# Nine of 49 destination blocks gathered, row turns in a layer's first steps, row stores on ScalarE's queue

## The chip, the cores and the metric

The kernel runs on one core of a Trainium2 chip. The metric is device time in microseconds, from the first to the last instruction of the program and what lies around them.

## What is computed

Four graph networks in a row over one graph of 6250 nodes (128 features) and 100000 edges, each behind a layer norm with relu and added to its input. The parts that matter here are the sums over edges:

```python
# L0: 2 layers, batch norm:   pooled = segment_sum(h[src'], dst', 6250) * inv_deg
# L1 ("sage"), 4 layers:
agg = jax.ops.segment_sum(h[src], dst, num_segments=N_NODES)
agg = agg / jnp.maximum(deg, 1.0)[:, None]
h = h @ Ws + agg @ Wn + b            # relu but in the last layer
# L2 ("plain" sum), 1 layer: messages = concat(nodes[senders], edge_attr) @ W_message.T
aggregated = jax.ops.segment_sum(messages, receivers, num_segments=n_nodes)
# L3 ("conv"), 2 layers, with self loops:
agg = jax.ops.segment_sum(ew[:, None] * (h @ W)[s], d, num_segments=n); h = elu(agg + b)
```

## The kernel before

The nodes are 49 blocks of 128 (NS), 6272 columns. `build_tables` writes a table of edge counts (8-bit, source block by source lane by destination) to memory. A sum over edges is then a dense product: the rows of the source nodes, split in two 16-bit parts (`rows`, kept on the chip), times the table's columns. L1, L2 and L3 do this in `layer_chain` (L2019), called three times: kind "sage" with L = 4 layers, "plain" with 1 and "conv" with 2. L0 runs outside it.

*Dense part.* Destinations are cut into strips of US = 7 blocks, 896 columns, done as two halves of 448 in banks 0 and 1 (`acc`). DENSE = 6 strips take the dense path. A strip goes through the 49 source blocks in 14 pieces (`PIECES`, 4 and 3 blocks in turn). `dense_piece` waits for the piece's DMA and does, for both halves, for each block, for both parts one product at L2139: 14 pieces are 196 products. SP loads pieces into a ring of five buffers (`load_piece`), each as its buffer comes free.

*Gathered part.* The last US = 7 blocks (from GB0 = 42) don't use the table. For each block there is a list of its edges' sources (`glist`), and a unit is a third of a block's list: GpSimd issues GH = 6 indirect DMAs (L2116), each fetching 128 rows of 512 bytes from `hrows`, a copy of the rows in memory, into one of two buffers (`grow`). VectorE writes a hot matrix for the unit (`hots`, L2278) that says to which of the 128 destinations each row belongs, also in two buffers. TensorE does 12 products of 128 columns (`gathered`, L2163) into banks 6 and 7. So there are 21 units (NGH) in a layer. `GATHER_AT` gives the strip and piece behind which a unit is done: pieces 1, 4, 7 and 10 of strips 1 to 5, and piece 13, the last, of strip 4. GpSimd waits for the unit two before to be used (`g_used`), and at a layer's start for all row stores (`hr_out`).

*What follows a strip.* VectorE takes a bank out (`leave_bank`, L2311, L2313), sage adds the own term that TensorE made in `own_term` (L2175, L2318), ScalarE writes the new features (`replace`, L2247). The gathered blocks are taken out in two portions of 4 and 3 blocks (`HALVES`, `LAST_S`), at strip 3 and at strip 5. Then the new rows for the next layer are made: `turn` (L2195) multiplies each block by the next weight, ScalarE writes the high part (`high`, L2238), VectorE the low part (`turned_in`, L2290). A strip is turned behind piece TURN_AT = 2 of the next strip (the last one: of the next layer's first strip), the gathered blocks behind piece 12 of strip 5. SP stores each strip's rows to `hrows` (`store_rows`, L1204) from its own queue, R + 2 = 7 pieces later than the turn.

All engines work through their own queues in order; the order is written out by hand, engine by engine. VectorE's order in a strip is: the previous strip's `turned_in`, then the hot matrices `units(s)[2:] + units(s + 1)[:2]`, then the portions, then `leave_bank` of the strip.

*Before a chain.* `split_rows` (L1208) makes the first rows. For sage and plain its SP queue loads the first five pieces and then stores the rows in four DMAs (`ROW_STORES`, 576 to 1024 KB). It is a block of its own: the next block, the chain, starts when all engines' queues are through. In sage, ScalarE loads a broadcast factor row of 3136 KB (`C<-factors`) once five pieces are used. For conv, `update_nodes` makes and stores the first rows, and the change leaves it alone.

Of the kernel before, what the change touches and what calls it, by code (L numbers as in the profile page):

```python
# [65 lines left out]
GB0 = (NU - 1) * US  # L66
# [4 lines left out]
NGH = GU * US  # L71
# [517 lines left out]
def build_tables(k):  # L589

    nc = k.nc
    with ExitStack() as own:
# [15 lines left out]
        excess = sb("excess_g", [P, US], F32)  # L608
# [12 lines left out]
        with nc.Block() as block:  # L621
# [29 lines left out]
            def _(dve):  # L651
# [36 lines left out]
                mine, after = (blocks[:, GB0 % 4 + i:GB0 % 4 + i + US] for i in range(2))  # L688
# [362 lines left out]
def product(k, terms, dst, func, bias, stats=False, tbuf=None, lists=False):  # L1051
# [3 lines left out]
    with nc.Block() as block:  # L1055
# [6 lines left out]
        if lists:  # L1062
            @block.gpsimd
            def _(pool):
# [3 lines left out]
                for n in range(US):  # L1068
# [85 lines left out]
def load_piece(k, sp, tbuf, s, i, slot=None):  # L1154
# [4 lines left out]
    sp.dma_start(tbuf[:, at:at + (hi - lo) * SU].rearrange("p (b u) -> p b u", u=SU),  # L1159
                 k.table[t * US + lo:t * US + hi, :, bass.ds(s * SU, SU)].rearrange("b l u -> l b u")  # L1160
# [47 lines left out]
def split_rows(k, v, over_src, at, weight, own, tbuf, keep, store=False):  # L1208
# [17 lines left out]
    with nc.Block() as block:  # L1226
        @block.sync
        def _(sp):
# [691 lines left out]
def elu_stage(k, sums, bias, dst, out=None):  # L1920
# [19 lines left out]
    with nc.Block() as block:  # L1940
# [26 lines left out]
        if out is not None:  # L1967
# [24 lines left out]
HALVES = [(0, 4), (4, US)]  # L1992
DENSE = NU - 1
LAST_S = NU - 1
CHUNKS = [(0, 0), (0, 1), (1, 0), (1, 1), (2, 0), (2, 1), (LAST_S, 0), (3, 0), (3, 1), (4, 0), (4, 1), (LAST_S, 1),
          (5, 0), (5, 1)]
TURNS = [0, 1, 2, 3, 4, LAST_S, 5]
TURN_AT, TURN_LAST_AT, OWN_AT = 2, 12, 12
GATHER_AT = {at: n for n, at in enumerate(sorted([(s, i) for s in range(1, DENSE) for i in (1, 4, 7, 10)] + [(4, 13)]))}


def chunk_of(s, q):

    if s < DENSE:
        return slice(s * STRIP + q * HALF, s * STRIP + (q + 1) * HALF)
    return slice((s * US + HALVES[q][0]) * P, (s * US + HALVES[q][1]) * P)


def chunk_width(s, q):

    return HALF if s < DENSE else (HALVES[q][1] - HALVES[q][0]) * P


def blocks_of(s, q):

    return [s * US + i for i in range(*HALVES[q])]


def layer_chain(k, kind, v, dst, layers, at_scale, tbuf, factor=None, out=None):  # L2019
# [5 lines left out]
    total, turns = L * DENSE * NH, (L - 1) * NU  # L2025
# [9 lines left out]
    turned = {(l, s): l * NU + j for l in range(L) for j, s in enumerate(TURNS)}  # L2035

    def count(l, s, q):

        return l * len(CHUNKS) + CHUNKS.index((s, q)) + 1

    def before(l, s, q):

        same = [(m, c[0]) for m in range(L) for c in CHUNKS if c[1] == q]
# [3 lines left out]
    def acc(s, q):  # L2047

        return k.bank[q if s < DENSE else 6 + q][:, 0:chunk_width(s, q)]

# [8 lines left out]
    def events(l, s):  # L2059

        first = (l, s - 1) if s else (l - 1, DENSE - 1)
        return ([first] if first[0] >= 0 else []) + ([(l, LAST_S)] if s == DENSE - 1 else [])

    with ExitStack() as own_space:
# [10 lines left out]
        with nc.Block() as block:  # L2075
            @block.sync
            def _(sp):
                stores = {}
                for l in range(L - 1):
                    for j, s in enumerate(TURNS):  # L2080
                        piece = (l * DENSE + DENSE - 1) * NH + TURN_LAST_AT if s == LAST_S else (
                            l * DENSE + s + 1) * NH + TURN_AT
                        stores[piece + R + 2] = (l, s)
                for n in range(R, total):
                    sp.wait_ge(used.h, used.at(n - R + 1))
                    load_piece(k, sp, tbuf, n // NH % DENSE, n % NH, n % R)
# [4 lines left out]
                for j, s in enumerate(TURNS if conv else ()):  # L2091
                    sp.wait_ge(o_copied.h, o_copied.at(2 * j + 2))
                    b1 = min((s + 1) * US, full)
                    sp.dma_start(out[s * STRIP:b1 * P, :].rearrange("(b p) f -> p b f", p=P),
                                 out_rows[:, s * US:b1, :]).then_inc(o_out.h, 16)
                    if s == LAST_S:
                        sp.dma_start(out[full * P:N, :], out_rows[0:N - full * P, full, :]).then_inc(o_out.h, 16)
                if conv:
                    sp.wait_ge(o_out.h, o_out.at(16 * (NU + 1)))

            @block.gpsimd
            def _(pool):
# [5 lines left out]
                for l in range(L):  # L2108
                    pool.wait_ge(hr_out.h, hr_out.at(16 * (len(ROW_STORES) + l * NU)))
# [11 lines left out]
            def _(pe):  # L2121
                T = nc.tensor

                def dense_piece(l, s, i):
# [3 lines left out]
                    slot = k.sem(f"table_in{n % R}")  # L2128
                    pe.wait_ge(slot.h, slot.at(16 * (n // R + 1)))
                    counts = tbuf[:, n % R * 4 * SU:(n % R + 1) * 4 * SU].bitcast(F8)  # L2130
                    for h in range(2):
                        if i == 0:
                            if l or s:
                                pe.wait_ge(acc_read.h, acc_read.at(count(*((l, s - 1) if s else (l - 1, DENSE - 1)), h)))
# [779 lines left out]
```

## Time and profile before

| | us |
|---|---|
| median of 3 runs | 3297.43 (3289.22 to 3302.65) |
| profiled execution, its own time | 3289.41 |
| its span, first to last instruction | 3287.7 |
| TensorE busy | 2952.4 (90%), 18657 products |
| of these the dense products L2139 | 1598.1, 8232 products |
| gathered products L2163 | 122.5, 1764 products |
| GpSimd busy | 1114.6 (34%), of it gathers L2116 940.5, 882 DMAs |
| VectorE busy | 1048.6 (32%) |
| ScalarE busy | 733.9 (22%) |
| DMA | 492.60 MB, mean 150 GB/s |

The chains of layers stand from 1225.2 to 2255.9 us (sage), 2327.7 to 2569 (plain) and 2758.8 to 3287.7 (conv). A row of the list of groups gives a source line, an engine, an operation and its tiles, then busy time, the mean of one, and the engine's idle time just before with what ended it. The mean of one product (353 ns) is longer than the time from one start to the next, since products overlap in the array; costs are therefore taken from start to start. The granted TensorE clock is given as a share of 2.4 GHz.

### The profile page before, as it was taken

The numbers are of one execution on the slowest core, as the hardware profiler recorded it, in microseconds if no ns is written. First come the engines' busy times: TensorE is split into PE (matmuls) and PEld (weight loads), VectorE is DVE, ScalarE is ACT, GpSimd is POOL, SyncE is SP. The second block draws the span as 40 slices with busy tenths as digits, with TensorE's granted clock in tenths as the row PEclk, the third lists the DMA queues.
The fourth block names the chain that finished last, engine by engine and source line by source line (L and its number), as shares of the span: only waits on it lengthen the run. The fifth ranks groups of instructions, "written<-read, shape, count | busy, mean of one in ns | idle before, by whom it ended". The sixth has DMA issues, their size and how long they took to land. (4 is left out here: it accounts for less than half of the span.)

```text
span 3287.7 us, 44136 instructions
## 1 busy us (share of the span) xinstructions
PE 2952.4 (90%) x18657; PEld 1749.1 (53%) x18657; DVE 1048.6 (32%) x1858; ACT 733.9 (22%) x1172; POOL 1114.6 (34%) x1012
## 2 busy tenths in 40 slices
PE   1799879996899879999999999998799767999998
PEld 1688735552444335555555555553455664555554
DVE  5899822223200261111111111114111463222122
ACT  4799812223100230000000000001000373111000
POOL 5000023330000004653562562661367001553564
PEclk9999989997899989999999999999899887999999
DMA  7244599993466226666666666662766103665665
GB/s 257 60 132 132 158 228 175 169 154 84 109 148 147 48 71 205 181 169 174 179 171 165 176 177 165 175 172 53 197 180 178 50 31 111 172 180 161 170 172 156
DMA packets 768366, 492.60 MB, mean 150 GB/s; under 512 B 362500, under 2 KB 749836, under 8 KB 767568
## 3 DMA queue, kind: packets, MB, share of 16 engines
q1 hardware_dynamic: 705362, 395.76, 49.7%
q0 software_dynamic: 30112, 62.69, 6.5%
q10 hardware_dynamic: 32702, 31.44, 3.0%
q8 instruction: 140, 2.29, 0.3%
q14 instruction: 50, 0.41, 0.0%
HBM read 334.89 MB, written 76.82 MB: 125 GB/s over the span
## 5 line engine op out<-in xcount | busy, mean ns | idle before, releaser
L2139 PE MATMUL acc<-tbuf,hs 128*128 128x448 fp8e4 x8232 | 1598.1, 353 | 24.6 <-PEq L1226 12.5
L2116 POOL DMA_INDIRECT grow<-hrows,glist x882 | 940.5, 1066 | 789.1 <-PE acc L2163 386.9
L2139 PEld LDWEIGHTS acc<-tbuf,hs 128*128 128x128 f16 x8232 | 800.3, 98 | 764.8 <-issue 52.1
L2278 DVE TENSOR_TENSOR edge_loc<-iota,gdl 128x768 f16<-128x768 bf16 x147 | 140.6, 971 | 747.0 <-PE acc L2163 708.8
L711 ACT ACTIVATE stage<-quad 128x784 fp8e4<-128x784 f32 x392 | 290.5, 828 | 8.1 <-PE quad L731 5.5
L1610 PE MATMUL acc<-tbuf,hs 128*128 128x512 fp8e4 (+1 forms) x1300 | 281.6, 370 | 11.6 <-DMA tbuf<-table 11.6
L731 PE MATMUL quad<-K,S 128*128 128x196 bf16 x1568 | 277.4, 250 | 15.7 <-DVE K L655 10.4
L735 PE MATMUL deg<-K,S 128*128 128x196 bf16 x1568 | 276.2, 247 | 0.0
L1484 PE MATMUL acc<-tbuf,hs 128*128 128x512 fp8e4 (+1 forms) x1300 | 266.8, 369 | 0.6 <-issue 0.6
L2247 ACT ACTIVATE H<-B,vectors 128x448 f32<-128x448 f32 (+2 forms) x56 | 37.4, 668 | 817.1 <-DVE B L2318 817.1
L1484 PEld LDWEIGHTS acc<-tbuf,hs 128*128 128x128 f16 x1300 | 123.5, 98 | 143.9 <-issue 3.5
L1610 PEld LDWEIGHTS acc<-tbuf,hs 128*128 128x128 f16 x1300 | 120.4, 99 | 137.8 <-issue 17.1
L655 DVE TENSOR_TENSOR K<-iota,win_key 128x2744 bf16<-128x2744 bf16 x112 | 177.0, 1580 | 0.0
L2313 DVE SCALAR_TENSOR_TENSOR B<-acc,scales,C 128x448 f32<-128x448 f32 (+1 forms) x84 | 57.2, 681 | 365.0 <-PE acc L2139 267.4
L731 PEld LDWEIGHTS quad<-K,S 128*128 128x128 bf16 x1568 | 151.9, 97 | 40.6 <-DVE K L655 40.5
L735 PEld LDWEIGHTS deg<-K,S 128*128 128x128 bf16 x1568 | 154.2, 98 | 0.2
L1069 POOL DMA_INDIRECT glist<-edge_pairs,gof x7 | 7.0, 1002 | 374.6 <-SPq L1055 372.8
L1628 DVE TENSOR_TENSOR Z<-iota,edge_loc 128x1024 bf16<-128x1024 bf16 x98 | 73.6, 769 | 174.9 <-PE acc L1592 127.7
L655 DVE TENSOR_TENSOR S<-iota,win_low 128x1792 bf16<-128x1792 bf16 x112 | 122.3, 1092 | 10.3 <-PEq L271 3.5
L2163 PEld LDWEIGHTS acc<-edge_loc,grow 128*128 128x128 f16 x1764 | 110.9, 98 | 24.5
L2163 PE MATMUL acc<-edge_loc,grow 128*128 128x128 f16 x1764 | 122.5, 219 | 0.0
L2250 ACT ACTIVATE B<-B,vectors 128x448 f32<-128x448 f32 (+2 forms) x28 | 18.7, 668 | 421.2 <-DVE H L2321 420.9
(300 smaller groups left out, 2019.5 us busy)
## 6 DMA issues: line engine op xcount, KB each, us to landing
tbuf<-table SPq DMA_DIRECT2D x294, 448.0 KB
tbuf<-table SPq DMA_DIRECT2D x294, 336.0 KB
table<-stage SPq DMA_DIRECT2D x6, 5488.0 KB
grow<-hrows,glist POOLq DMA_INDIRECT x882
hrows<-hs SPq DMA_DIRECT2D x28, 448.0 KB, 4.4
feat<-in_edge_attr_dram ACTq DMA_DIRECT2D x27, 448.0 KB, 6.8
C<-factors ACTq DMA_DIRECT2D x2, 3136.0 KB, 12.4
table<-stage SPq DMA_DIRECT2D x2, 2744.0 KB
```

What stands on the lines that cost most here:

```text
L655: return V.tensor_tensor(to.rearrange("p n (c t) -> p n c t", t=2), iota.rearrange("p (c t) -> p c t", t=2).unsqueeze(1).to_broadcast([P, ...
L711: A.activation(stage[:, b, :, to:to + 4 * WD].rearrange("p b (w d) -> p w b d", d=WD), pair[(h * NQUAD + q) % 3][:, :].rearrange("p (t c) ...
L731: mm = T.matmul(pair[quad % 3][:, at:at + NKEY], S[:, q, i, :], K[:, q, i, :], start=(w % 2 == 0), stop=True, skip_group_check=True)
L735: mm = T.matmul(deg[:, w % 2 * NKEY:(w % 2 + 1) * NKEY], S[:, q, i, :], K[:, q, i, :], start=(w == 0), stop=(u == NHALF * NBATCH - 1 and i ...
L1484: mm = nc.tensor.matmul(acc[h][:, 0:n * P], k.hs[:, j, part, :], counts[:, :, j // 2, :, j % 2], start=(j == 0 and part == 0), stop=(j == ...
L1610: mm = T.matmul(acc[g % 2][:, 0:n * P], k.hs[:, j, part, :], counts[:, :, j // 2, :, j % 2], start=(j == 0 and part == 0), stop=(j == NL - ...
L1628: V.tensor_tensor(Z[:, u % 2, :, :].rearrange("p n (c t) -> p n c t", t=2), k.iota[:, 0:EWIN].rearrange("p (c t) -> p c t", t=2).unsqueeze ...
L2116: g.indirect_dma_start(out=grow[:, n % 2, t, :], out_offset=None, in_=k.hrows[l % 2], in_offset=bass.IndirectOffsetOnAxis(k.glist[:, i // ...
L2139: mm = T.matmul(acc(s, h), rows[l % 2][:, g * US + r, part, :], counts[:, (r - lo) * STRIP + h * HALF:(r - lo) * STRIP + (h + 1) * HALF], ...
L2163: mm = T.matmul(to, grow[:, n % 2, t, part * P:(part + 1) * P], hot[:, n % 2, t, :], start=(not conv and i % GU == 0 and t == 0 and part = ...
L2278: V.tensor_tensor(hot[:, n % 2, :, :], k.iota[:, 0:P].unsqueeze(1).to_broadcast([P, GH, P]), k.gdl[:, i // GU, i % GU * GH:(i % GU + 1) * ...
L2313: V.scalar_tensor_tensor(dst[:, at], acc(s, q), scale(1, l), k.C[:, at], ALU.mult, ALU.mult).then_inc(acc_read.h, 1)
```

## The change

- The dense path takes strips of 7, 7, 7, 7, 6 and 6 blocks (`STRIP_BLOCKS`); the last two strips use products of 384 columns. Nine blocks (GB0 = 40) are gathered, in portions of 4, 4 and 1 (`GROUPS`), numbered 6, 7 and 8. A layer has 27 units, at the places in `UNITS_AT`; none is behind piece 13, the first is behind piece 8 of strip 0.
- The last strip of a layer is turned behind piece 0 of the next layer's first strip (piece 1 for conv), the other strips as before behind piece 2. The portions are turned at (2, 12), (5, 5) and (5, 12).
- ScalarE stores the rows of a strip or portion right after its turn, having waited for VectorE's part (`z_lo`). The four stores before a chain are ScalarE's first instructions in the chain, no longer SP's last in `split_rows`; the factor row follows them without its wait.
- VectorE and ScalarE go through a strip piece by piece like TensorE: VectorE writes the hot matrix of unit u + 2 where unit u stands, and takes a portion out at the unit that completes it.

The core of the diff:

```diff
+STRIP_BLOCKS = [7, 7, 7, 7, 6, 6]
+GROUPS = [4, 4, 1]
+NG = sum(GROUPS)
+GB0 = sum(STRIP_BLOCKS)
...
-HALVES = [(0, 4), (4, US)]
-DENSE = NU - 1
-LAST_S = NU - 1
...
-TURN_AT, TURN_LAST_AT, OWN_AT = 2, 12, 12
-GATHER_AT = {at: n for n, at in enumerate(sorted([(s, i) for s in range(1, DENSE) for i in (1, 4, 7, 10)] + [(4, 13)]))}
+DENSE = len(STRIP_BLOCKS)
+ORDER = [(0, 0), (0, 1), (1, 0), (1, 1), (6, 0), (2, 0), (2, 1), (3, 0), (3, 1), (4, 0), (4, 1), (7, 0), (8, 0), (5, 0),
+         (5, 1)]
+TURN_AT, OWN_AT = 2, 12
+PART_TURNS = {(2, 12): 6, (5, 5): 7, (5, 12): 8}
+UNITS_AT = [[8, 11], [0, 3, 4, 7, 10], [0, 1, 3, 5, 8, 11], [0, 3, 4, 7, 9], [0, 1, 3, 6, 9], [0, 1, 4, 7]]
+GATHER_AT = {at: n for n, at in enumerate((s, i) for s, places in enumerate(UNITS_AT) for i in places)}
+PART_DONE = {GU * sum(GROUPS[:i + 1]) - 1: DENSE + i for i in range(len(GROUPS))}
...
+    def turn_at(s):
+        return TURN_AT if s else (0 if sage else 1)
...
 # split_rows, SP
-            for a, b in ROW_STORES if store else ():
-                sp.wait_ge(lo_ok.h, lo_ok.at(b))
-                store_rows(k, sp, k.hs, 0, 4 * a, min(4 * b, NS))
...
 # layer_chain, SP
-                    if n in stores:
-                        l, s = stores[n]
-                        sp.wait_ge(z_lo.h, z_lo.at(2 * turned[l, s] + 2))
-                        store_rows(k, sp, rows[(l + 1) % 2], (l + 1) % 2, s * US, (s + 1) * US)
...
 # layer_chain, TensorE
-                                              counts[:, (r - lo) * STRIP + h * HALF:(r - lo) * STRIP + (h + 1) * HALF],
+                                              counts[:, (r - lo) * strip + h * half:(r - lo) * strip + (h + 1) * half],
...
 # layer_chain, ScalarE
+                    act.wait_ge(z_lo.h, z_lo.at(count(l, s, chunks_of(s)[-1])))
+                    store_rows(k, act, rows[(l + 1) % 2], (l + 1) % 2, PART_AT[s], PART_AT[s] + PART_BLOCKS[s])
...
+                if not conv:
+                    for r0, r1 in ROW_STORES:
+                        store_rows(k, act, k.hs, 0, 4 * r0, min(4 * r1, NS))
                 if factor is not None:
-                    act.wait_ge(used.h, used.at(R))
                     act.dma_start(k.C[:, :], k.factors[factor:factor + 1, :].to_broadcast([P, NP])).then_inc(row_in.h, 16)
...
 # layer_chain, VectorE
-                        for h in units(s)[2:] + units(s + 1)[:2]:
-                            hots(l, h)
...
+                            if (s, i) in GATHER_AT:
+                                u = GATHER_AT[s, i]
+                                if u in PART_DONE:
+                                    leave_bank(l, PART_DONE[u], 0)
+                                    if conv:
+                                        finish(l, PART_DONE[u], 0)
+                                n = l * NGH + u + 2
+                                if n < L * NGH:
+                                    hots(n // NGH, n % NGH)
+                        for q in range(2):
+                            leave_bank(l, s, q)
```

## Rows read from the trace of the kernel before

**Rows 1.** Busy time in windows, the three chain stretches: first window, then the sum.
```profile
1225.20:2255.90 1030.70, 1020.38 (x6109) 570.78 (x6110) 175.48 (x241) 62.33 (x96) 539.90 (x505) 1.00 0.63 174
...
sum 1800.90, PE 1773.70 PEld 989.36 DVE 318.03 ACT 104.09 POOL 948.51; mean PE 591.24 PEld 329.79 DVE 106.01 ACT 34.70 POOL 316.17
```

**Rows 2.** Waits of TensorE in sage, then plain: waiter, releaser: us, times, longest.
```profile
PE acc L2139 <- DVE B L2313: 7.0, 4, 1.7
PE acc L2139 <- DMA tbuf<-table: 3.3, 1, 3.3
...
PE acc L2139 <- PEq L1226: 2.4, 1, 2.4
...
PE acc L2139 <- PEq L1226: 10.2, 1, 10.2
```

**Rows 3.** Costliest groups, GpSimd's gathers: busy us, mean ns, idle us before, releasers.
```profile
L2116 POOL DMA_INDIRECT grow<-hrows,glist x882 | 940.5, 1066 | 789.1 <-PE acc L2163 386.9 <-issue 236.4 <-DMA hrows<-hs 165.0
```

**Rows 4.** Timeline of TensorE at the end of sage's fifth strip: start us, us, operation.
```profile
1442.08 5.46 PE L2139 MATMUL acc<-tbuf,hs 128*128 128x448 fp8e4 x28 [1.74 <-DVE B L2313]
1447.38 0.83 PE L2163 MATMUL acc<-edge_loc,grow 128*128 128x128 f16 x12
1448.05 3.19 PE L2139 MATMUL acc<-tbuf,hs 128*128 128x448 fp8e4 x16
```

**Rows 5.** Timeline where sage's second layer starts, TensorE first, then other engines and queues.
```profile
1481.83 1.67 PE L2175 MATMUL acc<-H,weights 128*128 128x448 f32 x4
1483.33 1.72 PE L2195 MATMUL acc<-weights,H 128*128 128x128 f32 x14
1484.89 10.76 PE L2139 MATMUL acc<-tbuf,hs 128*128 128x448 fp8e4 x56
1495.48 1.72 PE L2195 MATMUL acc<-weights,H 128*128 128x128 f32 x14
...
1488.95 0.67 ACT L2247 ACTIVATE H<-B,vectors 128x448 f32<-128x448 f32 x1 [0.58 <-DVE B L2318]
...
1502.95 0.49 SPq L1204 DMA_DIRECT2D hrows<-hs  x1
...
1507.42 1.00 POOL L2116 DMA_INDIRECT grow<-hrows,glist  x1 [40.27 <-DMA hrows<-hs]
```

**Rows 6.** Timeline where plain begins: VectorE, SP's queue, TensorE, GpSimd.
```profile
2310.57 8.84 DVE L1246 SCALAR_TENSOR_TENSOR hs<-acc,scales,hs 128x512 f16<-128x512 f32 x13 [7.78 <-ACT hs L1256]
...
2313.91 13.37 SPq L1204 DMA_DIRECT2D hrows<-hs  x4
...
2327.73 5.56 PE L2139 MATMUL acc<-tbuf,hs 128*128 128x448 fp8e4 x15 [10.17 <-PEq L1226]
...
2332.19 1.00 POOL L2116 DMA_INDIRECT grow<-hrows,glist  x1 [1.79 <-DMA hrows<-hs]
```

**Rows 7.** Windows, first 4.9 us of plain: busy us, then clock, DMA share, GB/s.
```profile
2327.70:2332.60 4.90, 4.87 (x14) 1.96 (x15) 1.83 (x2) 0.00 (x0) 3.07 (x2) 0.50 0.68 204
```

**Rows 8.** Timeline: a unit's last gather, a hot matrix on VectorE, the gather beside it.
```profile
1280.22 0.99 POOL L2116 DMA_INDIRECT grow<-hrows,glist  x1 [0.30 <-issue]
...
1284.04 0.96 DVE L2278 TENSOR_TENSOR edge_loc<-iota,gdl 128x768 f16<-128x768 bf16 x1 [3.78 <-PE acc L2163]
1284.27 1.59 POOL L2116 DMA_INDIRECT grow<-hrows,glist  x1 [3.06 <-PE acc L2163]
```

**Rows 9.** Packets of the software queue, 1283.2 to 1284.2: count, MB, share of 16 DMA engines.
```profile
q0 software_dynamic: 22, 0.03, 8.7%
```

**Rows 10.** DMA issues by line: count, KB each, median us from issue to landing.
```profile
C<-factors ACTq DMA_DIRECT2D x2, 3136.0 KB, 12.4
...
hrows<-hs SPq DMA_DIRECT2D x3, 1024.0 KB, 11.3
...
wins<-edge_pairs,offi POOLq DMA_INDIRECT x13, 3.9
...
glist<-edge_pairs,gof POOLq DMA_INDIRECT x7, 2.4
```

More of the change, by code:

```diff
@@ L687, in _ @@
                 dve.wait_ge(g_step.h, g_step.at(2))
-                mine, after = (blocks[:, GB0 % 4 + i:GB0 % 4 + i + US] for i in range(2))
+                mine, after = (blocks[:, i:i + NG] for i in range(2))
                 V.tensor_tensor(excess[:, :], after, mine, ALU.subtract).then_inc(g_step.h, 1)
@@ L1158, in load_piece @@
     at = slot * 4 * SU
-    sp.dma_start(tbuf[:, at:at + (hi - lo) * SU].rearrange("p (b u) -> p b u", u=SU),
-                 k.table[t * US + lo:t * US + hi, :, bass.ds(s * SU, SU)].rearrange("b l u -> l b u")
+    start, n = (s * SU, SU) if strips is None else (sum(strips[:s]) * P // 2, strips[s] * P // 2)
+    sp.dma_start(tbuf[:, at:at + (hi - lo) * n].rearrange("p (b u) -> p b u", u=n),
+                 k.table[t * US + lo:t * US + hi, :, bass.ds(start, n)].rearrange("b l u -> l b u")
                  ).then_inc(k.sem(f"table_in{slot}").h, 16)
@@ L1205, in store_rows, with split_rows @@
                  rows[:, b0:b1, :, :].rearrange("p b a f -> p b (a f)")).then_inc(k.sem("hr_out").h, 16)
-def split_rows(k, v, over_src, at, weight, own, tbuf, keep, store=False):
+def split_rows(k, v, over_src, at, weight, own, tbuf, keep):
     nc = k.nc
@@ L2024, in layer_chain @@
     R = k.ring
-    total, turns = L * DENSE * NH, (L - 1) * NU
+    total, turns, parts = L * DENSE * NH, (L - 1) * len(ORDER), len(PART_BLOCKS)
     sage, conv = kind == "sage", kind == "conv"
@@ L2128, in dense_piece @@
                     slot = k.sem(f"table_in{n % R}")
+                    strip, half = STRIP_BLOCKS[s] * P, STRIP_BLOCKS[s] * P // 2
                     pe.wait_ge(slot.h, slot.at(16 * (n // R + 1)))
@@ L2183, in turn @@
                         return
-                    pe.wait_ge(ready.h, ready.at(count(l, s, 1)))
-                    for q in range(2):
-                        if leaves and j > turns:
-                            pe.wait_ge(o_copied.h, o_copied.at(2 * (j - turns - 1) + q + 1))
-                        elif j:
-                            pe.wait_ge(z_lo.h, z_lo.at(2 * (j - 1) + q + 1))
+                    pe.wait_ge(ready.h, ready.at(count(l, s, chunks_of(s)[-1])))
+                    for q in chunks_of(s):
+                        last = before(l, s, q)
+                        if last is not None and last > turns:
+                            pe.wait_ge(o_copied.h, o_copied.at(last - turns))
+                        elif last is not None:
+                            pe.wait_ge(z_lo.h, z_lo.at(last))
                         for i, b in enumerate(blocks_of(s, q)):
@@ L2209, in _ @@
                             dense_piece(l, s, i)
-                            if i == TURN_AT:
-                                for e in events(l, s)[0:1]:
-                                    if e[1] != LAST_S:
-                                        turn(*e)
+                            if (l or s) and i == turn_at(s):
+                                turn(*strip_before(l, s))
                             if i == OWN_AT and sage:
@@ L2381, in layer_chain @@
               layer_summed=chunks if sage else 0, layer_moved=chunks if sage else 0,
-              layer_ready=chunks if sage or conv else 0, z_full=2 * turns, z_hi=2 * turns, z_lo=2 * turns,
-              hr_out=16 * (len(ROW_STORES) + turns), g_set=1, g_used=L * NGH, hot_ok=L * NGH, gdl_ok=1,
+              layer_ready=chunks if sage or conv else 0, z_full=turns, z_hi=turns, z_lo=turns,
+              hr_out=16 * (len(ROW_STORES) + (L - 1) * parts), g_set=1, g_used=L * NGH, hot_ok=L * NGH, gdl_ok=1,
               g_got0=16 * GH * (-(-L * NGH // 2)), g_got1=16 * GH * (L * NGH // 2))
@@ L2853, in network @@
             with table_buffer(k, True) as tbuf:
-                split_rows(k, H, True, 2, layers[0][1], None, tbuf, False, True)
+                split_rows(k, H, True, 2, layers[0][1], None, tbuf, False)
                 layer_chain(k, "sage", H, B, layers, 2, tbuf, factor=1)
@@ L2864, in network @@
         with table_buffer(k, True) as tbuf:
-            split_rows(k, H, True, 0, None, None, tbuf, False, not spilled)
+            split_rows(k, H, True, 0, None, None, tbuf, False)
             if spilled:
```

182 lines of the change are left out of this document (86 added, 96 removed).

## The prediction

> **What bounds the kernel now.** I read first the busy times of the three stretches that `layer_chain` runs in: together 1800.9 us, of which TensorE works 1773.7, at a granted clock of 1.00 in the longest [rows 1]. So TensorE is the bound in 1801 of 3287.7 us, and nothing outside these stretches is touched except the end of `split_rows`. Then the list of what TensorE waited for [rows 2]: four waits of 1.7 us for a bank (L2313) in sage's four layers and, alike, one in plain and two in conv, 3.3 us for a table piece, 10.2 us at a block's start. Last, what runs beside it and becomes longer: GpSimd's gathers, 882 of them, with 789 us of idle time in front, of which 387 us wait for TensorE to free a buffer [rows 3]. TensorE never waited for a gather.
>
> **Dense products.** One of 448 columns starts every 0.189 us: 28 take 5.30 us, from 1442.08 to the unit at 1447.38 [rows 4]; four blocks of a piece are 16 products, 3.03 us, three are 2.27 us. Its rate per column: a 128-column product comes every 0.056 us (12 in 0.67 us, from 1447.38 to 1448.05, the same group), so 320 columns more cost 0.134 us and 64 columns 0.0267 us. The two strips of six blocks use 384 columns: 7 layers x 2 strips x 196 products x 0.0267 = **-73.2 us**. A seventh strip's worth of blocks is not saved elsewhere, since 9 instead of 7 of 49 blocks leave the dense path and 40 of 42 stay: 2/42 of the dense time.
>
> **Gathered units.** 27 instead of 21 in each layer: 42 more x 0.67 us = **+28.0 us** on TensorE. Turns and own terms keep their columns (own terms 1.50 us a strip, a turn of 7 blocks 1.56 us, from start to start [rows 5]), so splitting nine blocks into 4, 4 and 1 costs nothing by itself.
>
> **The wait at a strip's end.** VectorE works in order, and before strip 4 is taken out of its bank it writes a hot matrix that needs the unit put behind strip 4's last piece. TensorE is through with that unit and stands 1.74 us, until 1442.08 [rows 4]. No unit follows piece 13 after the change, and VectorE's queue is written in TensorE's order. Sage's four are 7.0 us [rows 2], seven are **-12.2 us**. The new places behind pieces 0 and 1 are passed after the bank was read: nothing new is late there.
>
> **The turn in the first step.** The last strip's turn moves from step 2 to step 0 (1 for conv). It waits for ScalarE to have replaced the strip: two steps for each half on VectorE, then 0.67 us on ScalarE, and it is over 2.5 us into the next layer already today [rows 5], against a first piece of 3.03 us. Cost nothing; if that cover fails, at most 1 us for each of 4 boundaries. (Today's work ends at 1488.95 + 0.67 = 1489.62, and the layer starts at 1484.89 + 12 x 0.189 = 1487.16; VectorE is held till then by the turn of the last rows, which now comes a step earlier and is one block.)
>
> **Stores on ScalarE.** SP carries the row stores behind table pieces: turn at 1495.48, issue at 1502.95, gathers from 1507.42 [rows 5], 20 us into the layer. With ScalarE issuing right after VectorE (some 3 us after the turn begins: 1.34 us of products, then 0.6 us on either engine, by the 0.67 and 0.69 us rows of like tiles) and the same 4.5 us of landing, gathers can begin at 3.0 + 3 + 4.5 = some 10.5 us. What is queued behind ScalarE's new wait (z_lo, some 1.3 us) is only the strip's replacement, which is not due. At the start of the sage and plain chains the four stores are moved behind the block's barrier. Plain: SP needs 13.37 us to issue them, TensorE had finished and sat 10.17 us [rows 6], and then ran 4.9 us at 0.50 of the clock, 14 products that take 2.6 us at full clock [rows 7]. A barrier bound by VectorE (it ends at 2319.41 [rows 6]) leaves 2.4 us, as sage's has [rows 2]: -7.8 us, and -2.3 us of slow clock: **-10.1 us**. Sage: the stores now collide with table pieces and with the 3136 KB factor row, beside which TensorE already waited 3.3 us for a piece [rows 2]. The stores are as many bytes again, so bounds are 0 (the ring of five pieces hides them) and twice those 3.3 us more; I take **+2.5 us**.
>
> **What GpSimd must now deliver.** This is the part that decides. One unit is six gathers at a spacing of 1.30 us, 7.8 us. But where VectorE writes a hot matrix at the same moment, the gather takes 1.59 us [rows 8] instead of 1.00 [rows 6]. The mean over all is 1.066 us [rows 3]: 882 x 0.066 = 58 us, which is 0.6 us for some 100 of the 147 units. After its last instruction the data still come: a unit's last instruction ends at 1281.21 [rows 8], and 22 packets of the software queue are still moved between 1283.2 and 1284.2 [rows 9], before the next gather is issued; other indirect DMAs land 2.4 us (small) and 3.9 us (large) after issue, of which 1.0 us is the instruction [rows 10]. So landing lies between 1.4 and 3.0 us after GpSimd is done; I take 1.8.
>
> With TensorE's steps (3.03 and 2.27 us for a piece, 0.67 a unit, and the turns and own terms) I lay the 27 due times against GpSimd, which needs unit u-2's buffer back. In a sage layer unit 7 is due at 87.8 us from the layer's start, so its buffer is refilled from 88.8 to 96.9 and lands near 98.8, while unit 9 is due at 98.3; unit 10 follows 8.4 us on, near 107.2, and is due at 104.8 ((2,3) and (2,5) are only 5.9 us apart). The same happens at units 17, 20, 21 and 22. Sum 6 to 8 us of waiting a layer for sage and for conv, 17 to 24 us for plain, whose layer is 21 us shorter (no turns, no own terms) and whose gathers begin about 15 us into it instead of 4.5 [rows 6], as the stores have just been issued (3.1 MB, the rate at which the factor row lands [rows 10]). Against the dense path: 27 units x 8.1 us = 219 us of a layer of 252 us. Both bounds laid the same way: 7.8 us units landing in 1.4 us give 25 us over the seven layers, colliding units landing in 2.5 to 3 us give 65 to 87 us. At 1.8 us: **+55 us** (25 sage, 17 plain, 13 conv).
>
> One rule speaks to the 1.59 us. The row shows a `tensor_tensor` lengthening a gather's instruction by 0.6 us [rows 8]. The Trainium skill (SBUF — State Buffer, "Who interferes with whom") says that a `tensor_tensor` with two SBUF inputs contends only with GpSimd's reads, and that it did not stall descriptor generation in their probe. By that, units would cost 7.8 us at all places; this trace disagrees. The sum would then be near -33 instead of -10 us.
>
> **Sum.** -73.2 + 28.0 - 12.2 - 10.1 + 2.5 + 55 = -10 us against the profiled execution's 3289.4 us; the median of the runs is 8 us above that, so I carry the difference over: 3297.4 - 10 = **3287 us**.
>
> **Rivals.**
> - *Gathers in time.* VectorE's and GpSimd's writes rarely coincide once GpSimd runs without pause (a gather is issued every 1.30 us, a hot matrix lasts 0.96 us [rows 8]), and landing is short. Waits shrink to 25 to 32 us: -33 to -40 us, 3257 to 3264. For it: over a layer the chain has 219 us of work in 252 us. Against it: the places are uneven, and two units of three collide today. With no waits at all it is -65 us, 3232. Chance 0.33.
> - *GpSimd becomes the bound (slower).* If landing takes 3 us in the fuller queues and the first gathers of plain and sage start 20 us late (both lengthen each pinch), waits reach 95 to 100 us: +30 to +35, 3327 to 3332. It decides from 82 us of waiting on (above the sum's other -65 plus 0.5%). Place: units 9, 10, 17, 20 of each layer. For it: stores of rows landed in 11.3 us where tables were loading [rows 10]. Against: the DMA share is only 0.63. Chance 0.15.
> - *The strip ends keep their wait*, because a hot matrix still stands ahead of the bank on VectorE: 12.2 us come back, 3299. Against: no unit is left at piece 13. Chance 0.04.
> - Forecast as summed, 3272 to 3305 for itself: 0.48.
>
> **Range.** 3252 (gathers in time) to 3320 (87 us of waits and a start 8 us worse) leaves out about 0.1 on each side. Measurement tells about 0.5%, 16.5 us, from no change. Faster by more: the first rival whole and a little of the forecast, 0.37. Within: 0.46. Slower: 0.17.
>
> **What would show it.** TensorE rows of L2139 at 384 columns near 0.163 us from start to start; 2268 gathered products; no 1.7 us wait for a bank; GpSimd idle time for TensorE much below 387 us; a new wait "PE <- DMA grow", 40 to 70 us in total, most in (2,3), (2,5), (3,9), (4,3); plain starting near 2320 us at full clock, yet no shorter than before. The prediction is wrong if that wait is under 30 us or above 85, or if the bank wait stays.

## The result, and the profile after

The kernel after took 3477.73 us (3470.76 to 3497.53, four runs), the kernel before 3298.44 us beside it: ratio 1.0563, interval [1.0532, 1.0593], slower by some 180 us where 3287 us and a range of 3252 to 3320 us were forecast. But that number doesn't hold everywhere. The same kernel ran in five more sessions, on chips 4, 14, 11, 6 and 12: 3317.3, 3320.3, 3317.3 and 3320.0 us on the first four (1.0082 [1.0065, 1.0099] on chip 4, where before took 3291.9), and 3481.5 us on chip 12 (1.0507, before 3314.5). Which chip the first session had isn't known. So there are two questions: why +25 to +30 us where -10 was forecast, on four chips, and what adds 160 us on a fifth and in the first session. The profile of the first session and that of chip 4 are read side by side.

First the page of the first session: span, engines, then the groups (busy us, mean ns | idle us before, releaser). In the kernel after, L2151 is the dense product (L2139 before), L2177 the gathered one (L2163), L2127 the gather (L2116), L2327 takes a bank out (L2313) and L1231 is the end of `split_rows` (L1226).

```profile
span 3496.0 us, 45582 instructions
...
PE 3007.9 (86%) x19177; PEld 1795.3 (51%) x19177; DVE 1096.5 (31%) x1923; ACT 735.8 (21%) x1184; POOL 1382.1 (40%) x1266
...
L2151 PE MATMUL acc<-tbuf,hs 128*128 128x448 fp8e4 (+1 forms) x8232 | 1609.3, 353 | 80.5 <-issue 53.3
L2127 POOL DMA_INDIRECT grow<-hrows,glist x1134 | 1206.2, 1064 | 739.1 <-issue 314.5
L2151 PEld LDWEIGHTS acc<-tbuf,hs 128*128 128x128 f16 x8232 | 810.4, 100 | 811.0 <-issue 208.6
```

The same lines of chip 4's page:

```profile
span 3312.3 us, 45582 instructions
...
PE 2919.5 (88%) x19177; PEld 1779.1 (54%) x19177; DVE 1094.5 (33%) x1923; ACT 735.2 (22%) x1184; POOL 1365.1 (41%) x1266
...
L2151 PE MATMUL acc<-tbuf,hs 128*128 128x448 fp8e4 (+1 forms) x8232 | 1541.9, 345 | 8.8 <-DMA tbuf<-table 4.7
L2127 POOL DMA_INDIRECT grow<-hrows,glist x1134 | 1189.0, 1049 | 575.1 <-issue 329.1
L2151 PEld LDWEIGHTS acc<-tbuf,hs 128*128 128x128 f16 x8232 | 801.1, 98 | 675.9 <-issue 39.9
```

Against the page of before: TensorE's busy time fell from 2952.4 to 2919.5 us, yet the span rose by 24.6 us. The first session's page has 88 us more of busy time than chip 4's for the same 19177 products, and its weight loads stood 208.6 us "for issue", where 52.1 us is what before has and 39.9 us is chip 4's: TensorE waited for nothing that the profile can name.

TensorE's waits on chip 4 (waiter, releaser: us, times, longest), which answer to [rows 2]:

```profile
PE acc L2177 <- DMA grow<-hrows,glist: 72.5, 43, 3.8
...
PE acc L2151 <- DMA tbuf<-table: 4.7, 1, 4.7
...
PE acc L2151 <- PEq L1231: 4.0, 2, 2.2
```

And in the first session:

```profile
PE acc L2151 <- issue: 53.3, 95, 1.6
PE acc L2177 <- DMA grow<-hrows,glist: 50.9, 29, 5.0
...
PE acc L2177 <- issue: 37.3, 56, 1.8
...
PE acc L2151 <- DVE B L2327: 16.8, 6, 7.6
```

On chip 4 the one new wait is for gathers, 72.5 us in 43 places; the 1.7 us waits for a bank are gone, and plain's start waits 2 us instead of 10.2. In the first session 90 us of waits have no releaser.

Windows on chip 4, the three chains (busy us (and count) of TensorE, its weight loads, VectorE, ScalarE, GpSimd; then granted clock, DMA share, GB/s), which answer to [rows 1]:

```profile
1225.00:2273.80 1048.80, 1008.20 (x6414) 589.17 (x6412) 203.51 (x280) 63.91 (x103) 679.46 (x649) 0.99 0.64 176
2334.30:2586.00 251.70, 233.51 (x1500) 133.15 (x1500) 34.77 (x41) 0.00 (x0) 169.47 (x163) 0.99 0.64 177
2778.50:3312.30 533.80, 504.24 (x3230) 298.17 (x3228) 126.63 (x190) 42.40 (x76) 346.21 (x325) 0.98 0.61 168
```

From the first to the last dense product sage is 16.5 us longer than before (1048.8 for 1032.3), plain 10.7 (251.5 for 240.8) and conv 6.9 (520.9 for 514.0), while plain begins 60.7 us behind sage's last product instead of 70.1: 34.1 - 9.4 = 24.7 us. (Each is counted from the start of the first product to the start of the last.)

### The profile page after: what moved, and what is told of

Same layout as the page of the kernel before. It is cut to its first block and busy times, and to the rows that moved or that the text cites. A ratio compares the mean times of both kernels' runs of the same rounds, so it can differ in the third digit from the quotient of the medians.

```text
span 3496.0 us, 45582 instructions
## 1 busy us (share of the span) xinstructions
PE 3007.9 (86%) x19177; PEld 1795.3 (51%) x19177; DVE 1096.5 (31%) x1923; ACT 735.8 (21%) x1184; POOL 1382.1 (40%) x1266
## 5 line engine op out<-in xcount | busy, mean ns | idle before, releaser
L2151 PE MATMUL acc<-tbuf,hs 128*128 128x448 fp8e4 (+1 forms) x8232 | 1609.3, 353 | 80.5 <-issue 53.3
L2127 POOL DMA_INDIRECT grow<-hrows,glist x1134 | 1206.2, 1064 | 739.1 <-issue 314.5
L2151 PEld LDWEIGHTS acc<-tbuf,hs 128*128 128x128 f16 x8232 | 810.4, 100 | 811.0 <-issue 208.6
L2293 DVE TENSOR_TENSOR edge_loc<-iota,gdl 128x768 f16<-128x768 bf16 x189 | 181.1, 968 | 1068.9 <-remote 527.5
L2177 PE MATMUL acc<-edge_loc,grow 128*128 128x128 f16 x2268 | 170.5, 221 | 90.1 <-DMA grow<-hrows,glist 50.9
L2261 ACT ACTIVATE H<-B,vectors 128x448 f32<-128x448 f32 (+3 forms) x60 | 38.6, 643 | 861.0 <-DVE B L2332 667.3
L2177 PEld LDWEIGHTS acc<-edge_loc,grow 128*128 128x128 f16 x2268 | 143.8, 99 | 132.5 <-issue 107.6
L2327 DVE SCALAR_TENSOR_TENSOR B<-acc,scales,C 128x448 f32<-128x448 f32 (+3 forms) x90 | 58.5, 650 | 278.0 <-PE acc L2151 109.3
L2116 POOL MEMSET grow<- 128x3072 f16 x3 | 8.0, 2660 | 298.4 <-POOLq L2461 188.8
L659 DVE TENSOR_TENSOR S<-iota,win_low 128x1792 bf16<-128x1792 bf16 x112 | 122.2, 1091 | 10.1 <-PEq L275 3.5
```

Source lines behind the costliest of these rows:

```text
L659: return V.tensor_tensor(to.rearrange("p n (c t) -> p n c t", t=2), iota.rearrange("p (c t) -> p c t", t=2).unsqueeze(1).to_broadcast([P, ...
L2127: g.indirect_dma_start(out=grow[:, n % 2, t, :], out_offset=None, in_=k.hrows[l % 2], in_offset=bass.IndirectOffsetOnAxis(k.glist[:, i // ...
L2177: mm = T.matmul(to, grow[:, n % 2, t, part * P:(part + 1) * P], hot[:, n % 2, t, :], start=(not conv and i % GU == 0 and t == 0 and part = ...
L2293: V.tensor_tensor(hot[:, n % 2, :, :], k.iota[:, 0:P].unsqueeze(1).to_broadcast([P, GH, P]), k.gdl[:, i // GU, i % GU * GH:(i % GU + 1) * ...
L2327: V.scalar_tensor_tensor(dst[:, at], acc(s, q), scale(1, l), k.C[:, at], ALU.mult, ALU.mult).then_inc(acc_read.h, 1)
```

## Experiments

*The first four* ran on chip 1, each once and with one thing changed, before it was known that the first session's time doesn't return on most chips. Before took 3291.1 us there, as on the chips where after takes 3317 us, so they are compared with 3317 us. "Theory P, Q, G" in the expectations are explanations of the first session.

Units two or three pieces apart:

```diff
-UNITS_AT = [[8, 11], [0, 3, 4, 7, 10], [0, 1, 3, 5, 8, 11], [0, 3, 4, 7, 9], [0, 1, 3, 6, 9], [0, 1, 4, 7]]
+UNITS_AT = [[8, 11], [0, 2, 5, 7, 10, 12], [1, 4, 7, 9, 12], [1, 3, 6, 8, 11], [0, 2, 5, 8, 10], [0, 2, 4, 7]]
```

> The kernel after took 3477.7 us, 180 us more than before, and its trace shows TensorE going on and off in bursts of a few instructions, mostly behind places where gathered units stand one or two pieces apart. Only the places are changed: 27 units now stand two or three pieces apart. Theory P (close units starve TensorE, and the clock then falls to half): most of the 180 us go, 3290 to 3340 us. Theory Q (ScalarE's queue of row stores is the cause) and theory G (the number of gathers that GpSimd issues back to back, 1134 instead of 882, is the cause): 3440 to 3490 us, no more than the 50 us of waits for a gather to be won.

Measured: 3263.95 us, wait for gathers 32.3 us.

Stores of turned rows back on SP's queue (`stores[piece + R + 2]`, as before):

> The kernel after with the stores of turned rows back on SP's queue, seven pieces behind their turn, as before the change; the four stores ahead of a chain stay with ScalarE. Theory Q (the stores on ScalarE's queue disturb TensorE): 3290 to 3350 us. Theories P and G: gathers of a new layer start some 10 us later, so 3480 to 3530 us.

Measured: 3326.95 us, wait 78.9 us.

The kernel before with those stores on ScalarE:

```diff
+                    act.wait_ge(z_lo.h, z_lo.at(2 * turned[l, s] + 2))
+                    store_rows(k, act, rows[(l + 1) % 2], (l + 1) % 2, s * US, (s + 1) * US)
```

> The kernel before with one part of the change alone: ScalarE issues the stores of turned rows, behind a wait for VectorE's part. Theory Q: well slower than 3298 us, by 50 us or more, with half-speed stretches of TensorE's clock. Theories P and G: within 10 us of 3298 us.

Measured: 3294.05 us against 3291.08.

Three of six gathers:

```diff
-                        for t in range(GH):
+                        for t in range(GH if n < 2 else GH // 2):
...
-                    pe.wait_ge(g_got[n % 2].h, g_got[n % 2].at(16 * GH * (n // 2 + 1)))
+                    pe.wait_ge(g_got[n % 2].h, g_got[n % 2].at(16 * (GH + GH // 2 * (n // 2))))
```

> The kernel after, in which GpSimd issues only three of a unit's six gathers from the third unit on; the other rows of the buffer stay as they were, so sums of the nine gathered blocks are left incomplete. TensorE's products, their places and all waits stay. Theory G (GpSimd's back-to-back gathers and their queue): 3230 to 3290 us. Theory P (close units on TensorE): the waits for a gather go, 51 us, and no more: 3420 to 3440 us. Theory Q: the same 3420 to 3440 us.

Measured: 3229.62 us, no wait for gathers; again on another chip:

> The kernel after with three of a unit's six gathers left out from the third unit on, so that TensorE never waits for one; the sums of the gathered blocks are left incomplete. In a session like most, 3225 to 3235 us again, which with the 3291 us of before makes the sum of all terms but the waits, -65 us by the prediction. If the state of the sixth session comes back (before at 3307 us or more): 3400 us or more if any kernel with 27 units falls into it, 3240 to 3260 us if it takes the full 1134 gathers.

Measured on chip 5: 3228.12 us, ratio 0.9794 [0.9778, 0.9810], before 3296.09.

Three single changes, each meant to remove another cause, all seemed to remove the 160 us: the evenly placed units land even below theory P's range, SP's stores in Q's and the half gathers at G's edge, while the kernel before with ScalarE's stores speaks against Q. They can't all be the cause. The control settled it: the kernel after itself doesn't have the 160 us on another chip.

> The kernel after, unchanged, run again beside the next kernel. Three kernels that each differ from it in one thing alone (places of the units, queue of the stores, number of gathers) took 3264, 3327 and 3230 us, and none had the on-and-off pattern of TensorE. Theory F (the pattern comes from all three together and belongs to this program): 3460 to 3500 us again, with a large part of the chains' semaphore records missing. Theory S (the pattern comes from outside the program, in the session in which it was timed): 3275 to 3300 us, which is what the sum of the prediction gives, with a wait for gathers of 50 to 60 us.

Measured: 3317.26 us, 1.0082 [1.0065, 1.0099], wait 72.5 us. The time comes from outside the program, as theory S says, but both numbers lie above what S gave: the sum of the prediction misses something here too.

> The kernel with the 27 units two or three pieces apart, timed. Under both theories 3255 to 3275 us, 0.99 of the kernel before: the 32 us of waits for a gather in its trace are 20 to 25 us fewer than the change as made would have.

Measured on the same chip: 3266.2 us, 0.9929 [0.9912, 0.9946]. So the places of the units alone are worth 51 us. The stores on ScalarE's queue are worth some 10 us (3327 against 3317, a single run against other chips, but its sage and conv stretches are together 11 to 15 us longer than in all four traces of the kernel after) and, in a single run, nothing to be seen in the kernel before, where the first unit is due a strip later.

*Why the gathers are late.* Three kernels on chip 14, beside the kernel after; the first two ran once each.

> The kernel after, unchanged, in a third session. It took 3477.7 us (ratio 1.056) in the first and 3317.3 us (1.008) in the second, and only the first has TensorE's on-and-off pattern and lacks half of its semaphore records. Theory S (the pattern comes from the session): 3310 to 3325 us, or again the pattern, whatever the other kernels of this call do. Theory F (it belongs to this program but comes and goes by itself): both times may appear within this call.

Measured: 3320.25 us, 1.0091 [1.0071, 1.0111]. Its wait for gathers, in the whole and then in sage:

```profile
PE acc L2177 <- DMA grow<-hrows,glist: 69.2, 42, 4.0
```
```profile
PE acc L2177 <- DMA grow<-hrows,glist: 35.1, 21, 4.0
```

No hot matrices behind the first two of a chain:

```diff
-                                if n < L * NGH:
+                                if n < 2:
                                     hots(n // NGH, n % NGH)
...
-                    pe.wait_ge(hot_ok.h, hot_ok.at(n + 1))
+                    pe.wait_ge(hot_ok.h, hot_ok.at(min(n + 1, 2)))
```

> The kernel after, in which VectorE writes only the first two hot matrices of a chain; TensorE uses these for all units, so sums of the gathered blocks aren't the reference's. In the second session's trace a unit's gathers took 7.5 us where no hot matrix was written beside them and 8.1 us where one was, and TensorE waited 72.5 us for gathers. Theory V (VectorE's hot matrices make the gathers late): all units take 7.5 us, the wait falls to 30 to 45 us, 3275 to 3290 us. Rival (landing and the uneven places make the wait, the 0.6 us are absorbed): wait over 60 us, 3305 to 3317 us.

Measured: 3289.22 us, 31 us less; wait 48.9 us, 20 us less. Its group of gathers:

```profile
L2127 POOL DMA_INDIRECT grow<-hrows,glist x1134 | 1133.0, 999 | 604.6 <-issue 326.6
```

999 ns instead of 1049: a unit's six gathers take 7.5 us at nearly every place, where on chip 4 107 of 189 units had a lengthened gather among them and took 8.0 us in the mean. The wait is a little above what theory V said and far below the rival's 60. So the hot matrices make a part of the wait, but 49 us of it stay without them.

A ring of half buffers for sage and plain, conv unchanged:

```diff
-        grow = sb("grow", [P, 2, GH, 2 * P], F16)
+        grow = sb("grow", [P, RG, GH // 2, 2 * P], F16)          # RG = 4 if kind == "conv" else 5
...
+                            m = 2 * n + t // (GH // 2)
+                            if m >= RG and t % (GH // 2) == 0:
+                                pool.wait_ge(g_used.h, g_used.at((m - RG) // 2 + 1))
```

> The kernel after with a ring of five half buffers (of three gathers each) instead of two whole ones for sage and plain, so GpSimd can fetch the first half of a unit one unit earlier; conv keeps two. Theory B (the wait comes from having only two units in flight at uneven places): the pinches of 1.7 us go, that of unit 10 of a layer falls from 3.7 to some 1.5 us; wait 30 to 40 us with conv's 20 among it, 3275 to 3290 us. Rival (GpSimd's rate is the limit, 7.8 to 8.1 us a unit): the wait stays over 60 us, 3305 to 3317 us.

Measured: 3277.87 us. TensorE's wait for gathers in its sage, then in its conv:

```profile
PE acc L2180 <- DMA grow<-hrows,glist: 3.2, 3, 1.4
```
```profile
PE acc L2180 <- DMA grow<-hrows,glist: 19.1, 11, 3.4
```

In the kernel after the same list has 35.1 us in sage and 19.3 in conv, on the same chip. With one half unit more of lead sage's wait is all but gone, while conv, with its two buffers, keeps its own: a control within one run. The mean gather is 1044 ns as against 1053. So GpSimd's rate is not the limit in sage; the lead is.

One part of the change alone on the kernel before, the four stores as ScalarE's first instructions in the chain:

```diff
 # split_rows, SP
-            for a, b in ROW_STORES if store else ():
-                sp.wait_ge(lo_ok.h, lo_ok.at(b))
-                store_rows(k, sp, k.hs, 0, 4 * a, min(4 * b, NS))
...
 # layer_chain, ScalarE
+                if not conv:
+                    for r0, r1 in ROW_STORES:
+                        store_rows(k, act, k.hs, 0, 4 * r0, min(4 * r1, NS))
                 if factor is not None:
-                    act.wait_ge(used.h, used.at(R))
```

> The kernel before with one part of the change alone: the four row stores ahead of the sage and plain chains are ScalarE's first instructions in the chain, and the factor row follows without its wait. The step of the prediction: -10.1 us (plain's barrier -7.8, its slow clock -2.3) and +2.5 us for sage, so 3281 to 3287 us where before takes 3291. Rival (the stores collide with the table pieces as much as they save): 3288 to 3295 us.

Measured: 3282.4 us against 3290.79, 0.9974 [0.9964, 0.9985], -8.4 us where the prediction's step says -7.6.

Both cures together, on chip 11:

> Both cures together: units two or three pieces apart, and five half buffers for sage and plain. Evenly placed units alone leave 32 us of waits for gathers (3266 us), half buffers alone took 3278 us, and the kernel with half of the gathers, which never waits for them, 3230 us. Theory B (two buffers and uneven places make the waits): 5 to 15 us of waits are left, most in plain and conv, 3240 to 3255 us. Rival (GpSimd's rate is the limit in what is left): 3258 to 3266 us.

Measured: 3257.42 us, 0.9901 [0.9884, 0.9917], the fastest of all that compute the reference. It lies between theory B's range and the rival's, so the time doesn't decide between them. 27.1 us of waits are left where theory B said 5 to 15: 2.3 in sage, 17.0 in plain and 7.8 in conv. Plain's gathers are not started before the rows are stored and its layer is the shortest; whether its wait comes from that or from GpSimd's rate, no run here shows.

> The kernel after, unchanged, in a fourth session: 3310 to 3325 us if the first session's 3478 us was that session's own; 3460 us or more if it comes back, and then with TensorE's on-and-off pattern.

Measured: 3317.29 us, 1.0079 [1.0059, 1.0099].

*What makes the first session slower still.* The trace of the first session also lacks records: of the semaphore increments it holds 19312, where chip 4's holds 36958 and that of before 32754. The next kernel raises a spare semaphore at each dense or gathered product that raised none:

```diff
+                                if not (r == hi - 1 and part == 1):
+                                    mm.then_inc(extra.h, 1)
```

> The kernel after, in whose three chains every product of TensorE that raised no semaphore now raises a spare one, 9135 increments more that nobody waits for. The trace of the first session (3478 us) lacks half of the semaphore records and shows TensorE's products going on and off in steps of 0.71 us. Theory R (semaphore traffic, or the recording of it, holds TensorE up once there is too much of it): 3340 us or more, with on-and-off stretches and lost records. Theory S (something of that session alone that this load doesn't bring about): 3310 to 3325 us, all records there.

Measured: 3316.78 us, all records there (45942).

> The kernel after, unchanged, in a fifth session: 3310 to 3325 us, or, if the first session's state comes back, 3460 us or more.

Measured on the same chip 6: 3319.97 us. Then chip 12:

> The kernel after, unchanged, in a sixth session: 3310 to 3325 us, or 3460 us or more if the first session's state comes back.

Measured: 3481.46 us, 1.0507 [1.0447, 1.0566], with 19221 increments in the trace.

> The kernel with evenly placed units beside it: 3255 to 3275 us in a session like the last four. If the first session's state comes back, it tells whether close units are needed for it (3255 to 3275 us all the same) or not (3400 us or more).

Measured: 3449.4 us, 1.0410 [1.0362, 1.0459].

> Evenly placed units and half buffers on another chip: 3250 to 3265 us, in the first session's state 3400 us or more.

Measured: 3463.81 us, 1.0454 [1.0405, 1.0502]. The kernel before took 3314.45 us there, 18 to 24 us above its 3290 to 3296 us on the other chips. So it came back with every kernel of 27 units that ran on chip 12, and close places are not needed for it. All runs on that chip are of one session, so chip and session can't be told apart there. The kernel with half of the gathers didn't run on it.

One trace speaks against taking the lost records for the cause. The kernel with half of the gathers has 28331 increments in its trace of chip 1 and 23021 in that of chip 5, a fifth fewer, and took 3229.62 and 3228.12 us: there records were lost and no time was, and TensorE shows none of the waits "for issue" in its chains.

How it looks, at unit 21 of sage's first layer. First chip 4's timeline of TensorE (start, us, operation), then the first session's at the same place in the program, then three windows of the latter (TensorE busy (products), granted clock, DMA share, GB/s):

```profile
1435.17 0.83 PE L2177 MATMUL acc<-edge_loc,grow 128*128 128x128 f16 x12 [1.42 <-DMA grow<-hrows,glist]
1435.84 2.44 PE L2151 MATMUL acc<-tbuf,hs 128*128 128x384 fp8e4 x14
```

```profile
1452.84 0.27 PE L2177 MATMUL acc<-edge_loc,grow 128*128 128x128 f16 x2
1453.74 0.38 PE L2177 MATMUL acc<-edge_loc,grow 128*128 128x128 f16 x4 [0.63 <-issue]
1455.17 0.33 PE L2177 MATMUL acc<-edge_loc,grow 128*128 128x128 f16 x3 [1.04 <-issue]
1456.59 0.22 PE L2177 MATMUL acc<-edge_loc,grow 128*128 128x128 f16 x1 [1.10 <-issue]
1457.30 0.28 PE L2177 MATMUL acc<-edge_loc,grow 128*128 128x128 f16 x2 [0.48 <-issue]
1458.72 0.48 PE L2151 MATMUL acc<-tbuf,hs 128*128 128x384 fp8e4 x1 [1.14 <-issue]
```

```profile
1456.20:1459.60 3.40, 1.15 (x5) 0.80 0.19 55
1459.60:1463.00 3.40, 3.20 (x10) 0.50 0.54 162
1463.00:1466.40 3.40, 3.40 (x16) 0.69 0.72 212
```

The twelve gathered products, 0.67 us on chip 4, come in groups of one to four that start, from the second group on, 0.7 or 1.4 us after one another, each idle time "for issue". From this unit's start to the next one's it is 15.9 us instead of 7.3. The DMA share falls to 0.19 meanwhile, so it isn't the DMA engines that are busy. Afterwards the clock is 0.50 and 0.69 in the two windows: a hold-up is paid twice. By my count over the chains of the first session's trace such gaps between dense or between gathered products hold 130 us more than on chip 4, the half-speed products behind them 49 us more, and 22 us of waits for gathers are saved since GpSimd catches up: 157 of 182 us. All of it lies in the chains. Of what is between and outside them the two traces agree within 2 us in sum.

## Why the prediction was wrong, step by step

**What bounds.** Right: the time is TensorE's in the chains, and outside them nothing moved but the barrier.

The step that failed is the term for the gathers' wait: the landing time in it was too short, and the slow clock behind the waits was put at nothing. The 160 us of the first session come on top and were in no step.

**The sum without waits** was right. Its terms other than the gathers' +55 are -73.2 + 28.0 - 12.2 - 10.1 + 2.5 = -65 us. The kernel with half of the gathers, whose traces have 1.0 and 3.5 us of waits for them, took 61.5 us less than before on one chip and 68.0 us less on another. One by one: a product of 384 columns comes every 0.1625 us (forecast 0.163), as 12 of them between these starts of chip 4's timeline show:

```profile
1457.75 2.11 PE L2151 MATMUL acc<-tbuf,hs 128*128 128x384 fp8e4 x12
1459.70 0.83 PE L2177 MATMUL acc<-edge_loc,grow 128*128 128x128 f16 x12
```

The bank waits are gone, and the barrier measured by itself gave -8.4 us for -7.6. Plain's first 4.9 us on chip 4 hold 26 products at full clock, where [rows 7] has 14 at half:

```profile
2334.30:2339.20 4.90, 4.90 (x26) 1.00 1.12 334
```

**The wait for gathers** is the term that was mis-sized: forecast 55 us (25 in sage, 17 in plain, 13 in conv), measured 72.5 us by the list of waits (35.8, 18.2, 18.5), and 79 us as gaps in front of units, counted from start to start (39, 20, 20). The mechanism and the places were as forecast: of the gaps 21.5 us are at a layer's unit 10, 17.2 at unit 20, 11.0 at unit 17, 9.7 at unit 9, 5.5 at unit 21. What was mis-sized in it is the landing. GpSimd around units 9 and 10 on chip 4 (start, us), then TensorE:

```profile
1319.10 1.59 POOL L2127 DMA_INDIRECT grow<-hrows,glist  x1 [1.95 <-PE acc L2177]
...
1326.54 1.00 POOL L2127 DMA_INDIRECT grow<-hrows,glist  x1 [0.30 <-issue]
1327.84 0.99 POOL L2127 DMA_INDIRECT grow<-hrows,glist  x1 [0.31 <-issue]
...
1334.83 1.00 POOL L2127 DMA_INDIRECT grow<-hrows,glist  x1 [0.30 <-issue]
```

```profile
1329.22 0.83 PE L2177 MATMUL acc<-edge_loc,grow 128*128 128x128 f16 x12 [0.60 <-DMA grow<-hrows,glist]
...
1338.86 0.83 PE L2177 MATMUL acc<-edge_loc,grow 128*128 128x128 f16 x12 [3.51 <-DMA grow<-hrows,glist]
```

Unit 9's last gather ends at 1327.54 and TensorE starts on it at 1329.22, 1.7 us later. Unit 10's ends at 1335.83, and TensorE, idle since about 1335.4, starts at 1338.86, 3.0 us later. Over the 43 places of the list the mean is 2.4 us. I had bounds of 1.4 to 3.0 us and took 1.8 for all; with 2.5 to 3 us at such places my own upper working gives 65 to 87 us. Taken together the 43 places lie some 27 us above 1.8 us each, enough for the 17.5 us that were missing, but no run changes the landing alone. I took the value nearest to a small, lone transfer [rows 9, 10]. What lengthens it stays open: a unit right before is not enough, since unit 17 follows its predecessor after the same 0.3 us as unit 10 does and was usable 2.2 to 2.3 us after its last gather in all seven layers, where unit 10 took 2.3 to 3.1 us. The unit's length of 7.8 or 8.4 us with a pause was right. The sign that I had named missed the failure: 72.5 us is above the 40 to 70 us expected but below the 85 us at which the prediction was to be wrong.

**The clock** was missing. I took slow clock off at plain's start [rows 7] and never added it behind the new waits. Windows behind the gap at 1338.86 (columns as above):

```profile
1339.90:1343.20 3.30, 3.30 (x10) 0.50 0.15 40
1345.40:1350.00 4.60, 4.60 (x32) 1.00 0.79 217
```

Ten products in 3.3 us at half speed, then full speed again. Products that come at about twice their distance add 14 us of slow clock in chip 4's trace, 18 to 23 us in those of chips 6, 11 and 14, and 4 to 6 us in those of the half gathers; so the waits of 79 us cost some 9 to 18 us more. The granted clock says the same: it is at half for 29 us of chip 4's chains, for 39 to 50 us on chips 6, 11 and 14, for 9 and 13 us with half gathers and for 8 us in before's. And each cure won more time than waits: 31 us for 20 without hot matrices, 42 for 34 with half buffers, 51 for 39 with even places. -65 + 79 + 9 = +23, measured +25 in the two profiled executions (3314.1 and 3289.4).

**The rivals.** "Gathers in time" (0.33) fell. "GpSimd becomes the bound", 95 to 100 us of waits, was given 0.15 and is nearest to what the four chips show: its point of decision, 82 us beyond the -65, was reached by 79 us of waits and their clock together. Its landing of 3 us is what unit 10 had, but GpSimd as the bound isn't right: sage's waits went with half a unit of lead, at the same rate of GpSimd. The times on the four chips lie at the upper edge of the range, chip 14's 0.3 us outside; the sign of the forecast was wrong on all.

**The rule on interference.** I had set the trace against the Trainium skill (SBUF — State Buffer, "Who interferes with whom"), by which VectorE's `tensor_tensor` should not hold up GpSimd's descriptor work, with the sum at -33 instead of -10. The run without hot matrices decides for the trace: on the same chip the mean gather fell from 1053 to 999 ns, the waits by 20 us and the time by 31 us. But the passage, as the prediction gives it, leaves room for contention with GpSimd's reads, and each gather reads its row numbers from `glist`, which lies in SBUF: that units cost 7.8 us at all places doesn't follow from it. Whether this read is what is held up, no run here shows.

**The chip.** The 160 us of the first session were in no rival, and nothing in the trace of before pointed to them. What stays open is the cause. Shown: it doesn't come from the program alone but with a chip or a session; it holds TensorE up in steps of 0.7 us; semaphore records were lost in all four traces that have it, but chip 5 lost a fifth of them without it; over their times elsewhere it cost before up to 24 us, the kernel after 164, the evenly placed units 183 and those with half buffers 206; 24% more increments on chip 6 bring nothing. The Trainium skill (NOTIFIC — the notification-queue block, "Overflow: three behaviours, one of which stalls the engine") says of this block, which writes the records, that when the ring of a queue is full it either discards records or holds back the engine that produces them, as the queue is set. Each sign alone fits a recording path that is slower there, but no run here shows it, nor whether the 160 us would be there without the recording: it would need before's trace, or the half gathers, on chip 12.

## What to carry to other kernels

Where one engine feeds another through two buffers, lay out its rate and its lead separately: half a buffer more took 32 us of waits from sage, evenly spread places took 51 us off the kernel, and neither changed the rate. Size the landing of a transfer by a loaded place, not by a lone one (2.4 us in the mean where TensorE waited, 1.8 taken), and add the slow clock that follows a wait of TensorE. And before explaining a surprising time, run the same kernel on another chip: here some 150 of the 180 us were gone on four of five.

## What the runs showed of the hardware that was not expected

- One of six chips (1, 4, 6, 11, 12, 14) ran kernels with 27 units of six gathers 4 to 5% slower than before, which itself lost only 0.7%; a first session, on a chip not known, was 5.6% slower. In the traces of both TensorE starts in steps of 0.71 us, mostly for stretches of 1 to 11 us.
- A trace can lose a fifth of its semaphore records with no time lost (23021 of 28331 on chip 5, 3228.12 us against 3229.62).
- A gather of 128 rows of 512 bytes takes 1.00 us of GpSimd alone and 1.33 to 1.59 us beside a `tensor_tensor` of 0.97 us. Where TensorE waited on chip 4, a unit's data were usable 1.7 to 3.8 us after its last gather ended, 2.4 us in the mean.
- One idle time of 3.5 us of TensorE was followed, 1.0 us after its end, by 3.4 us at 0.50 of the clock.
